# Attention's start, the last stage and the Newton steps of a four-stage transformer kernel

## The reference

```python
x = _layernorm(x + _L0_attn_ref(x, ...))   # state space mixer, 2 heads
x = _layernorm(x + _L0_ffn_ref(x, ...))    # gelu feed-forward, 1024 hidden
x = _layernorm(x + _L1_attn_ref(x, ...))   # causal linear attention, 16 heads of 16, 64 features each
x = _layernorm(x + _L1_ffn_ref(x, ...))    # 2 shared experts and top 2 of 8 experts
```

```python
qkv = x @ Wqkv + bqkv
xn = x / jnp.maximum(jnp.linalg.norm(x, axis=-1, keepdims=True), 1e-12)     # for q and k, per head
arg = jnp.clip(proj * sqrt_2s - s, -20.0, 20.0)                             # proj = xn with omega, s = quad_nodes
feat = jnp.exp(arg) / np.sqrt(M) * sqrt(quad_weights)
out = ctx / den @ Wout + bout
```

## Time and profile before

| | us |
|---|---|
| median of 3 runs | 1658.53 (1656.6 to 1659.21) |
| the profiled execution | 1657.14 |
| its span | 1655.5 |
| PE busy | 1415.1 (85%) |
| DVE busy | 934.4 (56%) |
| ACT busy | 679.9 (41%) |
| POOL busy | 509.5 (31%) |

### The profile page before, as it was taken

One profiled execution on the slowest core, in us unless ns is written; L12 is line 12 of the kernel. 1 busy time (PEld: TensorE's weight loads), 2 busy tenths in 40 slices (PEclk: granted clock), 3 DMA queues, 4 the chain that ended last, 5 costly groups with the idle time before them and its releaser, 6 DMA issues. The chain is left out here.

```text
span 1655.5 us, 34268 instructions
## 1 busy us (share of the span) xinstructions
PE 1415.1 (85%) x12248; PEld 1219.7 (74%) x12248; DVE 934.4 (56%) x2089; ACT 679.9 (41%) x1252; POOL 509.5 (31%) x395
## 2 busy tenths in 40 slices
PE   6799999717998897987988489999997999999980
PEld 5687878605666675665766388888886999999970
DVE  4866665435767657666676425543434555555545
ACT  2456566412434343343433233222223555555541
POOL 0234433301243332333410000643302444444440
PEclk9799999957999899899989699999998999999995
DMA  6234321030032131322200630424218888888866
GB/s 240 80 122 136 134 83 46 13 132 13 2 128 75 65 114 38 127 76 70 82 26 27 225 148 26 142 90 150 68 51 210 235 232 239 237 230 238 240 141 203
DMA packets 107783, 204.25 MB, mean 123 GB/s; under 512 B 18496, under 2 KB 81344, under 8 KB 101440
## 3 DMA queue, kind: packets, MB, share of 16 engines
q1 hardware_dynamic: 79248, 143.88, 26.7%
q0 software_dynamic: 23088, 54.31, 11.4%
q10 hardware_dynamic: 5376, 5.13, 0.9%
HBM read 144.72 MB, written 58.55 MB: 123 GB/s over the span
## 5 line engine op out<-in xcount | busy, mean ns | idle before, releaser
L2080 PE MATMUL e_ps<-e_xhl,e_whl 128*128 128x256 f32 x1872 | 249.3, 283 | 3.6 <-DMA e_whl<-wlo 3.5
L2080 PEld LDWEIGHTS e_ps<-e_xhl,e_whl 128*128 128x128 f32 x1872 | 234.0, 190 | 4.1 <-issue 4.1
L1669 PE MATMUL d_ps<-d_xhl,d_whl 128*128 128x512 f32 x768 | 192.0, 399 | 5.4 <-DVE d_whl L1740 5.4
L1669 PEld LDWEIGHTS d_ps<-d_xhl,d_whl 128*128 128x128 f32 x768 | 143.3, 192 | 34.5 <-issue 5.7
L1977 POOL DMA_INDIRECT xs<-e_y,e_slot_id x78 | 121.5, 1558 | 83.0 <-ACT e_y L2007 68.1
L1215 ACT ACTIVATE c_qf<-c_cf,c_fc 128x512 f32<-128x512 f32 x64 | 46.1, 721 | 229.7 <-DVE c_cf L1337 229.7
L2060 PE MATMUL e_ps<-e_whl,e_ghl 128*128 128x256 f32 x936 | 137.7, 283 | 0.5 <-DVE e_ghl L2155 0.5
L345 POOL TENSOR_TENSOR b_hhl<-b_h,b_hhl 128x512 fp32r<-128x512 f32 x64 | 85.5, 1339 | 157.3 <-ACT b_hhl L572 125.1
L2143 DVE TENSOR_TENSOR e_g<-e_ps,e_act_h 128x256 f32<-128x256 f32 x156 | 66.3, 425 | 115.6 <-ACT e_act_h L2021 115.5
L2060 PEld LDWEIGHTS e_ps<-e_whl,e_ghl 128*128 128x128 f32 x936 | 120.5, 188 | 0.7 <-ACT e_ghl L2031 0.7
L1844 DVE TENSOR_TENSOR d_g<-d_ps,d_act_h 128x512 f32<-128x512 f32 x64 | 44.3, 692 | 123.8 <-PE d_ps L1669 89.5
(11 more groups left out here) (307 smaller groups left out, 2667.5 us busy)
## 6 DMA issues: line engine op xcount, KB each, us to landing
e_whl<-wlo SPq DMA_DIRECT2D x39, 1024.0 KB, 5.0
e_whl<-wlo SPq DMA_DIRECT2D x39, 512.0 KB
c_eraw<-in_expert_w POOLq DMA_DIRECT2D x24, 512.0 KB, 4.7
wlo<-c_elo POOLq DMA_DIRECT2D x24, 512.0 KB, 3.0
wall<-in_expert_w SPq DMA_DIRECT2D x8, 1536.0 KB, 8.2
xg<-b_zeros POOLq DMA_DIRECT2D x13, 780.0 KB, 4.3
e_xr<-xg SPq DMA_DIRECT2D x39, 260.0 KB, 3.6
b_xts<-in_x_t SPq DMA_DIRECT2D x14, 512.0 KB, 5.4
```

The lines of the kernel that those rows point to most:

```text
L1669: mm = pe.matmul(ps[:, H + 2 * (m % 2) + w, :], whl[:, wp, e, lo:lo + P], xhl[:, k, xp, kd, :], start=q == 0, stop=q == 3 * KD - 1)
L2080: mm = pe.matmul(ps[:, H + m, w * SLOT:(w + 1) * SLOT], whl[:, k, wp, lo:lo + P], xhl[:, k, xp, kd, :], start=q == 0, stop=q == 3 * KD - 1)
```

## The change

Three parts of the kernel are edited.

1. `rsqrt` and `norm_newton`: a Newton step is three operations, two of them scalar_tensor_tensor (two tensors and a constant).

```diff
     for n in range(3):
-        chain.link(ve.tensor_tensor(t, r, r, ALU.mult))
+        chain.link(ve.scalar_tensor_tensor(t, r, -0.5, r, ALU.mult, ALU.mult))
         chain.link(ve.tensor_tensor(t, t, v, ALU.mult))
-        chain.link(ve.tensor_scalar(t, t, -0.5, 1.5, ALU.mult, ALU.add))
-        ins = ve.tensor_tensor(r, r, t, ALU.mult)
+        ins = ve.scalar_tensor_tensor(r, t, 1.5, r, ALU.add, ALU.mult)
```

```diff
             sp.dma_start(raw[:], wqkv.rearrange("p k n -> p (k n)")).then_inc(s["raw_in"], 16)
...
             sp.dma_start(xr[:], x2[0]).then_inc(s["x_in"], 16)
-            sp.wait_ge(s["raw_lo"], 1)
-            sp.dma_start(raw[:, 0:KD * D], wout.rearrange("p k n -> p (k n)")).then_inc(s["raw_in"], 16)
-            sp.wait_ge(s["raw_lo"], 2)
-            sp.dma_start(raw[:, 0:PAIRS * P], omega.rearrange("p k n -> p (k n)")).then_inc(s["raw_in"], 16)
+            sp.dma_start(ids[:], ident).then_inc(s["ids_in"], 16)
+            sp.dma_start(bq[:], bqkv.partition_broadcast(P)).then_inc(s["bias_in"], 16)
+            sp.dma_start(ns[:, 0], nodes.rearrange("p o -> (p o)").partition_broadcast(P)).then_inc(s["nodes_in"], 16)
+            sp.dma_start(nw[:, 0:1], nodes).then_inc(s["nodes_in"], 16)
+            sp.dma_start(nw[:, 1:2], weights).then_inc(s["nodes_in"], 16)
+            sp.dma_start(omr, omega.rearrange("p k n -> p (k n)")).then_inc(s["omega_in"], 16)
+            sp.dma_start(tri[:], masks[0]).then_inc(s["weights_in"], 16)
+            sp.dma_start(wor, wout.rearrange("p k n -> p (k n)")).then_inc(s["wout_in"], 16)
+            sp.dma_start(bo[:], bout.partition_broadcast(P)).then_inc(s["weights_in"], 16)
             sp.dma_start(xb[:], x2[0]).then_inc(s["res_in"], 16)
...
-            pe.wait_ge(s["weights_in"], WEIGHTS)
-            pe.wait_ge(s["raw_lo"], 4)
-            pe.wait_ge(s["fc_ready"], 2)
+            pe.wait_ge(s["ids_in"], 16)
             everything(pe, body)
```

TensorE waits for the low part of Wqkv before the first FQ and for all four low-part steps before the first `features`. GpSimd and VectorE wait for `weights_in` (now mask and output bias) in the bodies 1 and 0. On ScalarE the high part of Wqkv comes first; `other_weights` (Ln for the query bias, high parts of Wout and omega) comes behind turn 2 of `body(-1)`. On VectorE the order in `body(-1)` is:

```diff
             ve.wait_ge(s["raw_hi"], 1)
+            low(wq[:, 1].rearrange("p k n -> p (k n)"), raw[:], wq[:, 0].rearrange("p k n -> p (k n)"))
+            node_scales()
...
                     ins.then_inc(s["x_free"], 1)
+                    if first(i):
+                        if (name, a) == ("FT", 1):
+                            node_roots()
+                            ve.wait_ge(s["bias_in"], 16)
+                        if (name, a) == ("FQ", 0):
+                            scale_omega()
+                        if (name, a) == ("FQ", 1):
+                            query_bias()
+                        if (name, a) == ("FQ", 3):
+                            other_weights()
```

```diff
-        QUARTER = STEPS // 4
+        ACT_B, DVE_B = (5, 7), (4, 6)
...
+            act.wait_ge(scales_ready, 1)
+            for i in range(HALF):
+                apply(i)
+            act.wait_ge(scales_ready, 2)
+            for n, i in enumerate(ACT_B):
+                apply(i)
+                act.wait_ge(by_act, HALF + n + 1)
+                act.dma_start(out[i], o[:, bb(i)]).then_inc(stored, 16)
...
+            scales(0)
+            scales(1)
+            ve.wait_ge(scales_ready, 2)
+            for i in DVE_B:
+                for b in range(BATCH):
+                    t = i * BATCH + b
+                    last = ve.tensor_scalar(o[:, t, :], x[:, t, :], small[:, 3, t:t + 1], small[:, 5, t:t + 1], ALU.mult, ALU.add)
+                last.then_inc(by_dve, 1)
...
+    def in_rows(ap):
+        return ap.rearrange("(c p b) d -> c p b d", b=BATCH, p=P)
...
-        phase_combine(nc, views(xs[0:TILES * P]), views(flat(out)))
+        phase_combine(nc, in_rows(xs[0:TILES * P]), in_rows(flat(out)))
```

More of the change, by code:

```diff
@@ L94, in rsqrt @@
             chain.link(ins)
-RSQRT_LINKS = 14
+RSQRT_LINKS = 11
 def wait(eng, sem, value):
@@ L891, in phase_attention @@
         PAIRS_ALL = PAIRS * STEPS
-        WEIGHTS = 16 * 7
+        WEIGHTS = 16 * 2
+        omr = z[:].rearrange("p b d -> p (b d)")
+        wor = out[:].rearrange("p b d -> p (b d)")[:, 0:KD * D]
         A_, B_, C_ = range(3)
@@ L907, in is_step, with first @@
             return not isinstance(n, int) or 0 <= n < STEPS
+        def first(i):
+            return isinstance(i, int) and i == -1
         def step_of(i, name, a):
@@ L1083, in x_step @@
                 elif name == "FQ":
+                    if first(i) and a == 0:
+                        pe.wait_ge(s["raw_lo"], 1)
                     mm = split3(ps[:, xp, :], lambda p, kd: xts[:, p, kd, a * P:(a + 1) * P], lambda p, kd: wq[:, p, kd, 0:2 * D], KD)
@@ L1119, in features @@
                 wait(pe, "clip_done", n)
+                if isinstance(i, int) and i == 0 and t == 0:
+                    pe.wait_ge(s["raw_lo"], 4)
                 rows = [slice(2 * HD * at, 2 * HD * (at + 1)) for at in (t % 4, (t + 1) % 4)]
@@ L1242, in body @@
                 for t in range(PAIRS):
+                    if isinstance(i, int) and i == 0 and t == 0:
+                        act.wait_ge(s["fc_ready"], 2)
                     if pair(i, t, 0) is not None:
@@ L1251, in body @@
                     x_high(i, t, C_)
+                    if first(i) and t == 2:
+                        other_weights()
                     if 1 <= t <= EPER and (not isinstance(i, int) or 1 <= i < LAST):
@@ L1411, in body @@
                         norm_newton(norm, False)
+                    if isinstance(i, int) and i == 0 and t == 1:
+                        ve.wait_ge(s["weights_in"], WEIGHTS)
                     if pair(i, t, 1) is not None:
@@ L2184, in _ @@
                 sp.dma_start(x[:, bb(i)], xs[i]).then_inc(x_in[i], 16)
-            for n, i in enumerate(range(0, STEPS, 2)):
-                sp.wait_ge(by_act, n + 1)
+            for i in range(HALF):
+                sp.wait_ge(by_act, i + 1)
+                sp.dma_start(out[i], o[:, bb(i)]).then_inc(stored, 16)
+            for n, i in enumerate(DVE_B):
+                sp.wait_ge(by_dve, n + 1)
                 sp.dma_start(out[i], o[:, bb(i)]).then_inc(stored, 16)
@@ L2191, in _, with apply @@
         def _(act):
+            def apply(i):
+                for b in range(BATCH):
+                    t = i * BATCH + b
+                    last = act.activation(o[:, t, :], x[:, t, :], ACT.Identity, bias=small[:, 5, t:t + 1], scale=small[:, 3, t:t + 1])
+                last.then_inc(by_act, 1)
             for i in range(1, STEPS, 2):
                 act.dma_start(x[:, bb(i)], xs[i]).then_inc(x_in[i], 16)
-            for h in range(2):
-                act.wait_ge(scales_ready, h + 1)
-                for i in range(4 * h, 4 * h + 4, 2):
-                    for b in range(BATCH):
-                        t = i * BATCH + b
-                        last = act.activation(o[:, t, :], x[:, t, :], ACT.Identity, bias=small[:, 5, t:t + 1], scale=small[:, 3, t:t + 1])
-                    last.then_inc(by_act, 1)
-                for i in range(4 * h + 1, 4 * h + 4, 2):
-                    act.wait_ge(by_dve, i // 2 + 1)
-                    act.dma_start(out[i], o[:, bb(i)]).then_inc(stored, 16)
+            act.wait_ge(scales_ready, 1)
+            for i in range(HALF):
+                apply(i)
[4 more added lines that the diff above has]
+                act.dma_start(out[i], o[:, bb(i)]).then_inc(stored, 16)
         @block.vector
@@ L2207, in _, with scales @@
             ch = Chain(ve, own, 0)
-            for h in range(2):
-                for i in range(4 * h, 4 * h + 4):
+            def scales(h):
+                for i in range(HALF * h, HALF * (h + 1)):
                     ve.wait_ge(x_in[i], 16)
```

99 lines of the change are left out of this document (47 added, 52 removed).

## The result

The changed kernel took 1607.65 us (median of 4 runs, 1606.5 to 1610.8) beside 1657.57 for the kernel before: a ratio of 0.970, 95% interval 0.9684 to 0.9715. The profiled execution took 1607.56 us, 1606.0 of it span.

| stretch | before | after | difference | forecast |
|---|---|---|---|---|
| mixer, up to attention's first load | 335.2 | 323.2 | -12.0 | -3.0 |
| attention's start, up to its first feature product | 55.9 | 38.4 | -17.5 | -16.9 |
| attention's loop and end | 534.3 | 518.6 | -15.8 | -7.7 |
| shared stage | 321.4 | 323.3 | +1.9 | 0 |
| experts | 372.4 | 371.9 | -0.5 | 0 |

A forecast was written before the change was run, and what follows sets the result against it. TensorE, busy 85%, idles in attention's start and the last stage, chains of loads, VectorE and ScalarE. 16.9 + 5.3 + 0.6 + 1.2 + 6.5 + 2.4 = 32.9 us off 1657.1 gives 1624.2, put at 1625; range 1613 to 1637.

The forecast's parts named there:

- Attention's start: Loads and splits in order of need bring the first feature product sooner: 16.9 us gained, bounds 14 and 20.
- the interference with GpSimd at both places: Attention's start: GpSimd's squares stretch the second query-bias operation and meet the two low parts; 3.5 us late, bounds 1.25 and 4.6.
- The last stage: New order of statistics and scales gains 3.6 us, 4 KB rows 1.7: 5.3 together, bounds 3.6 and 6.5.
- A layer norm loses 0.6: Every layer norm: three Newton steps each lose one small link of 0.2 us, 0.6 us in all.
- Six times 0.4: 2.4, bounds 0 and 5: Mixer's steps: shorter norms cut TensorE's six waits, 4.0 us in all, for the activation behind the norm; 2.4 us gained.
- up to 6 x 1.2 + 0.6: Attention's steps: both norms' savings pass to TensorE, up to 7.8 us; 6.5 taken, bound below 0.
- The head norm's share: Attention's 128-column head norm: three shorter Newton steps save 0.78 or 0.42 us; 0.6 taken.
- rival 2: Whole kernel: no POOL-VectorE meeting, all of part 3 passes, one half-clock stretch spared: 1615 us; chance 0.13.
- rival 5: Whole kernel slower: TensorE falls to half clock in new places, 4 us a stretch, 1665 us at ten; chance 0.04.
- rival 1: Loops keep their time, another wait ending at the same place; loses the 6.5 and 2.4: 1634 us; chance 0.23.
- rival 3: Last stage: 4 KB rows bring nothing, by the skill's rule: 1627 us; chance 0.07.
- rival 4: Attention's start keeps its length through a late omega or node load, all but 2 us: 1640 us; chance 0.03.

The follow-up runs named there:

- e1: Kernel before with only the mixer's layer norm given three-operation Newton steps: 1651.3 us, ratio 0.9939.
- e4: Kernel before with only the last stage as changed (order of statistics, 4 KB rows, three-operation Newton steps in its norms): 1650.6 us, ratio 0.9950.
- e11: Changed kernel with the last stage's loads and stores in 1 KB rows as before: 1615.1 us, ratio 0.9737.
- e10: Kernel before with only attention's head norm given three-operation Newton steps: 1657.4 us, ratio 0.9995.
- e3: Kernel before with only attention's start as changed, in the order of need: 1639.7 us, ratio 0.9887.
- e9: Kernel before with only attention's row norm given three-operation Newton steps: 1646.5 us, ratio 0.9926.
- e6: Changed kernel with two more chained operations in the mixer's layer norm, 13 links for 11: mixer 326.9 us, 323.2 in the changed kernel.
- e15: Changed kernel with four-operation Newton steps back in attention's row norm alone, 14 links: 1621.7 us, ratio 0.9769.
- e18: Changed kernel with three more chained operations in attention's row norm, 14 links: 1634.9 us, ratio 0.9723.

## Why the prediction was wrong

The misses add up as 49.5 - 32.9 = 16.6 us of the span: 9.0 in the mixer, 8.1 in attention's loop, 0.6 in the start, 0.3 in the last stage, and 1.4 the other way in the stages that no edit touches, whose time moves by 2 to 3 us between kernels anyway (321.9 to 324.9 for the shared stage in e1 to e4, on one chip, which all have it unchanged). By the means over several kernels, 2 us each of the mixer's 9.0 and the loop's 8.1 are chance, and 7 and 6 are missed.

- **Attention's start: right, step by step** (16.9 for 17.5). The queue, the interference with GpSimd at both places, and the shorter norm are there with their sizes. It missed the table load, 1.3 us on the way to the first exponential, behind the point at which the forecast stopped counting.
- **The last stage: right** (5.3 for 5.6), and by e11 and e4 both halves of it too.
- **"A layer norm loses 0.6"** was the count of links and right as that. **"Six times 0.4: 2.4, bounds 0 and 5" failed** in the mixer. I sized it by TensorE's wait for ScalarE, and TensorE was not what a step was waiting for. ScalarE waited for the scales 1.4 to 2.0 us in five steps, and its activations feed TensorE and GpSimd for the whole next step. An operation at that chain's end, mostly the last, stood under GpSimd's next operation, so in five of six intervals 0.6 us of links took about another 1.1 us with them. The earlier trace rows is such a collision in a mixer step, the earlier one of the two (246.58; the one that is spared follows at 249.38); I used it for the start and did not follow the chain in which it was found to its end. The bound of 5 was no bound, since it counted what links cost and not what they meet.
- **Attention's steps, "up to 6 x 1.2 + 0.6": the mechanism was right and the term mis-sized.** TensorE's wait at the step's end did take the row norm's 0.6 us one for one. The head norm's share, which I had at the same size, shows as 0.7 to 0.8 in e10's like intervals, though not in its median. What was missing is the clock: waits of 3.0 us in every second step cost 2.7 us more behind them; behind 0.8 that is gone, and behind 2.4 it is at most 1.6. I had this row (2.98 us, 26 matmuls in 4 us), priced such a stretch at 4 us, and put it into rival 2 as one stretch spared, when the trace showed one in every second step (and not "at every step's end", as rival 5 has it). Part of it (3.4 us, or 4.7 against the mean of the old loops) even came with the start alone: in e3 one listed wait was 2.97 and the others 1.4 to 1.5.
- **Rival 2** (more than the sum, 1615) was the right side with the wrong first reason: GpSimd and VectorE do meet in the start. **Rival 5** (slower through the clock) had the same mechanism with the sign turned; shorter waits made fewer stretches, as its "against" said. Rivals 1, 3 and 4 are out by e1 and e9, by e11, and by the ledger.

Open: why the loop's time still differs by 6 us between profiles of one kernel's loop (half-clock stretches lie at other places, and no run here fixes where), and why the median of e10 shows nothing of the head norm's share.

## What to carry to other kernels

Price a shorter chain at its end, not by its length: find who starts when it ends (here ScalarE, with the next step's work behind it), and look at what the chain's last operations stand under in time; a link that moves them from behind another engine's start to ahead of it is worth that engine's whole operation. Vary the chain by single links on both sides of the change: small even costs with one jump show the collision and its margin, 0.02 us in the step shown of e6, and say how easily the next edit loses it. Where TensorE's clock falls behind some of a loop's waits, count every place with such a wait, compare intervals with like waits, and compare whole loops by several profiles.

## What the runs showed of the hardware

- A GpSimd operation on SBUF also holds up a VectorE operation with a single SBUF input: 1.10 us for a 128x128 TENSOR_SCALAR that takes 0.23. The reduction of 128x1024 from SBUF that began beside the same GpSimd operation took 1.22, and 1.20 to 1.22 in all 16 places of the changed kernel, so not every operation pays.
- The waiting is for the whole operation however small one's own is: one column took 1.89 us beside a 1.89 us square. GpSimd pays too: 3.38 us in place of 1.3 beside a scan of 2.29 us.
- A scalar_tensor_tensor on 128 columns of SBUF took 0.29 us, as a tensor_tensor did; the 0.343 of the earlier trace rows has one input in PSUM.
- 4 KB rows moved 406 GB/s, 1 KB rows 351, in the same loads of the same stage.
- TensorE's mean clock in the 4 us behind a wait was 1.00 behind 0.8 and 1.43 us (e15, 53 matmuls), 0.71 behind 2.35, and 0.51 behind 2.96 (24 matmuls); in e18 it was 0.70 behind 1.43 once, and in e15 it was at half behind 1.67 and 1.37, so the wait alone doesn't settle it.
